# A ternary feed-forward kernel: w2 transposed by two DMAs in place of TensorE

## What is computed

```python
q_emb = relu(cond @ W3 + b3)                    # (128, 256)
v_sum = sum(x, axis=1, keepdims=True)           # over the 32 positions
c = relu((32 * x + v_sum) * q_emb[:, None, :] @ W2 + b2)
def ternary_quant(w):                           # s: mean of |w| over the whole matrix
    return clip(round(w / s), -1, 1) * s
h1 = c @ ternary_quant(w1).T                    # w1, w3: 682 x 256
h3 = c @ ternary_quant(w3).T
out = x + (silu(h1) * h3) @ ternary_quant(w2).T # w2: 256 x 682
```

## Time and profile before

| what | value |
|---|---|
| median of 3 runs | 171.23 us (171.2 to 171.48) |
| the profiled execution's own time | 171.47 us |
| its span, first to last instruction | 169.3 us |
| granted TensorE clock, mean | 0.997 of full speed |
| busy share of the span: TensorE / VectorE / ScalarE / GpSimd | 97% / 67% / 51% / 23% |
| DMA: bytes, mean rate | 14.25 MB, 84 GB/s |

### The profile page before, as it was taken

How to read it: one execution, slowest core, us unless ns; L and a number is a source line. 1 busy time by engine, 2 the same in 40 slices (tenths; PEclk the granted TensorE clock), 3 DMA queues, 4 the chain that set the end, 5 groups by cost and what they waited for, 6 DMA issues and landing times.

```text
span 169.3 us, 2525 instructions
## 1 busy us (share of the span) xinstructions
PE 164.0 (97%) x918; PEld 139.3 (82%) x918; DVE 113.7 (67%) x182; ACT 87.0 (51%) x161; POOL 38.1 (23%) x38
## 2 busy tenths in 40 slices
PE   7799999999999999999999999999999999999993
PEld 2788778888788887888788887888788888888792
DVE  3239997774994399664994389664995359356763
ACT  4159876636553463635553463635553475255540
POOL 5000022731506042410506042410506030000000
PEclk9999999999999999999999999999999999999998
DMA  4998659964065002620056002100030003000303
GB/s 136 310 361 123 100 79 327 349 131 64 0 166 82 4 0 98 117 33 0 0 145 99 8 0 89 38 0 0 2 126 4 0 2 124 0 4 0 124 0 124
DMA packets 36244, 14.25 MB, mean 84 GB/s; under 512 B 25904, under 2 KB 35976, under 8 KB 36232
## 3 DMA queue, kind: packets, MB, share of 16 engines
q1 hardware_dynamic: 35944, 13.90, 31.7%
q10 hardware_dynamic: 288, 0.20, 0.4%
HBM read 9.90 MB, written 4.19 MB: 83 GB/s over the span
## 4 chain that ended last, share of the span: by engine, by line
PE 93%; DMA 2%; SPq 1%; ACT 1%; DVE 1%; issue 0%; ACTq 0%
PE bank L464 48%; PE bank L493 25%; PE bank L394 17%; DMA xo<-in_x_dram 2%; PE bank L380 2%; PE bank L418 0%; PE bank L400 0%; DVE x L545 0%; ACT silu L343 0%; ACT T L304 0%; DVE xo L656 0%; SPq L195 0%; SPq L190 0%; SPq L192 0%; PE bank L406 0%
## 5 line engine op out<-in xcount | busy, mean ns | idle before, releaser
L464 PE MATMUL bank<-c_hi,T 128*128 128x512 f32 (+1 forms) x176 | 71.0, 403 | 0.2 <-ACT T L308 0.2
L464 PE MATMUL bank<-c_lo,T 128*128 128x512 f32 (+1 forms) x176 | 69.4, 394 | 0.0
L343 ACT ACTIVATE silu<-bank,checked 128x512 f32<-128x512 f32 (+1 forms) x48 | 33.0, 688 | 67.0 <-PE bank L464 67.0
L643 DVE TENSOR_TENSOR gf<-silu,bank 128x512 f32<-128x512 f32 (+1 forms) x48 | 32.8, 683 | 41.4 <-PE bank L464 32.4
L464 PEld LDWEIGHTS bank<-c_hi,T 128*128 128x128 f32 (+1 forms) x176 | 32.8, 186 | 6.8 <-ACT T L308 0.6
L464 PEld LDWEIGHTS bank<-c_lo,T 128*128 128x128 f32 (+1 forms) x176 | 32.8, 187 | 6.3
L253 POOL TENSOR_TENSOR c_lo<-ct,c_hi 128x512 fp32r<-128x512 f32 x12 | 20.6, 1714 | 71.2 <-ACT c_hi L294 71.2
L493 PE MATMUL bank<-T,g_hi 128*128 128x256 f32 x160 | 33.7, 289 | 0.0
L493 PE MATMUL bank<-T,g_lo 128*128 128x256 f32 x160 | 32.6, 281 | 0.0
L394 PE MATMUL bank<-x,W_sb 128*128 128x256 f32 x128 | 30.9, 384 | 0.1
L650 DVE TENSOR_TENSOR g_lo<-gf,g_hi 128x512 fp32r<-128x512 f32 x40 | 31.0, 776 | 0.0
(11 more groups left out here) (60 smaller groups left out, 75.1 us busy)
## 6 DMA issues: line engine op xcount, KB each, us to landing
out_dram<-xo SPq DMA_DIRECT2D x15, 256.0 KB, 2.3
xb<-in_x_dram SPq DMA_DIRECT2D x48, 64.0 KB, 2.6
xo<-in_x_dram SPq DMA_DIRECT2D x6, 512.0 KB, 8.1
w_sb<-in_L_ffn_w_dram SPq DMA_DIRECT2D x2, 640.0 KB
xo<-in_x_dram SPq DMA_DIRECT2D x4, 256.0 KB, 4.5
w_sb<-in_L_ffn_w_dram SPq DMA_DIRECT2D x1, 682.0 KB, 9.4
W_sb<-in_L_cond_W_dram SPq DMA_DIRECT2D x1, 256.0 KB, 3.2
out_dram<-xo SPq DMA_DIRECT2D x2, 128.0 KB, 2.1
```

Of the source, the lines that this page charges most:

```text
L343: nc.scalar.activation(silu[r, m % 2, :], h1[j % 2][r], ACT.Silu, scale=checked[r, 0:1]).then_inc(silu_done, 1)
L464: last = pe.matmul(dst[j % 2][0:w, :], T13[:, k, col:col + w], part[:, g % NC, k, :], start=(i == 0), stop=(i == len(passes) - 1))
L643: nc.vector.tensor_tensor(gf[r, m % 3, :], silu[r, m % 2, :], second, ALU.mult).then_inc(g_done, 1)
```

## The change

`transpose_w2` goes from TensorE. ScalarE issues two DMAs with transposition in its place (`turn_w2`), one for each half of the 256 outputs, right behind the signs of w1 and w3 and ahead of `silu_step(1)`. They read `w2_t`, now padded to 768 columns, and write `w2_T`, a new buffer in SBUF. GpSimd clears the 86 columns of the padding once, early. `signs_of_T2` waits for both DMAs, reads `w2_T` in three activations, not four, and stands behind `hi_step(1)`, not behind `hi_step(0)`. `above_w2_limit` is `above_limit` for the padded buffer, with as many elements.

```diff
@@ -71,7 +71,9 @@
         w2_sb = sb("w2_sb", [P, DC, H], F32)
         w1_t = sb("w1_t", [P, STEPS, D], BF16)
         w3_t = sb("w3_t", [P, STEPS, D], BF16)
-        w2_t = sb("w2_t", [P, DC, H], BF16)
+
+        w2_t = sb("w2_t", [P, DC, STEPS * P], BF16)
+        w2_T = sb("w2_T", [P, STEPS, D], BF16)
         abs_sums = sb("abs_sums", [P, 3], F32)
         scales = sb("scales", [P, 3], F32)
         limits = sb("limits", [P, 3], F32)
@@ -123,7 +125,6 @@
 
         w13_ps = [[bank[:, 2 * k + part, :].bitcast(BF16)[:, 0:DC * PART * P].rearrange("p (c n) -> p c n", c=DC)
                    for part in range(2)] for k in (1, 2)]
-        w2_ps = [bank[:, 4 + b, :].bitcast(BF16) for b in range(2)]
 
         def mixed_of(n):
             return bank[:, 0 if n % 2 else 6, :]
@@ -148,7 +149,7 @@
         ternary_done = sem("ternary_done")
         checked_done = sem("checked_done")
         early_hi_done, early_lo_done = sem("early_hi_done"), sem("early_lo_done")
-        wT_done = sem("wT_done")
+        w2_filled, w2_turned = sem("w2_filled"), [sem(f"w2_turned{c}") for c in range(DC)]
         part_done = sem("part_done")
         T1_copied, T3_copied, T2_copied = sem("T1_copied"), sem("T3_copied"), sem("T2_copied")
         mixed_done, xT_done, vsum_done, y_done, x1_done = sem("mixed_done"), sem("xT_done"), sem("vsum_done"), sem("y_done"), sem("x1_done")
@@ -239,6 +240,7 @@
             nc.gpsimd.tensor_copy(ident16[:], ident[:]).then_inc(const_ready, 1)
             nc.gpsimd.memset(ones[:], 1.0).then_inc(const_ready, 1)
             nc.gpsimd.memset(T2[:, HC, :].bitcast(F32), 0.0).then_inc(zeroed, 1)
+            nc.gpsimd.memset(w2_t[:, :, H:STEPS * P], 0.0).then_inc(w2_filled, 1)
             nc.gpsimd.memset(g_rest[:].bitcast(F32), 0.0).then_inc(zeroed, 1)
 
             def scale_by_q(n):
@@ -308,19 +310,19 @@
                     nc.scalar.activation(T13[:, :, rest:rest + HR2], w13_ps[k][part][:, :, whole * P:whole * P + HR2],
                                          ACT.Sign).then_inc(copied, 1)
 
+            def turn_w2():
+                act.wait_ge(ternary_done, 5)
+                act.wait_ge(w2_filled, 1)
+                for c in range(DC):
+                    act.dma_start(w2_T[:, :, c * P:(c + 1) * P], w2_t[:, c, :], transpose=True).then_inc(w2_turned[c], 16)
+
             def signs_of_T2():
-                act.wait_ge(wT_done, 1)
                 act.wait_ge(zeroed, 4)
-                nc.scalar.activation(T2[:, 0:W2_HALF, :],
-                                     w2_ps[0][:, 0:W2_HALF * D].rearrange("p (j d) -> p j d", d=D), ACT.Sign
-                                     ).then_inc(T2_copied, 1)
-                nc.scalar.activation(T2[:, W2_HALF:HC, :],
-                                     w2_ps[1][:, 0:(HC - W2_HALF) * D].rearrange("p (j d) -> p j d", d=D), ACT.Sign
-                                     ).then_inc(T2_copied, 1)
+                for c in range(DC):
+                    act.wait_ge(w2_turned[c], 16)
+                nc.scalar.activation(T2[:, 0:HC, :], w2_T[:, 0:HC, :], ACT.Sign).then_inc(T2_copied, 1)
                 for row in (0, HR2):
-                    nc.scalar.activation(T2[row:row + HR, HC, :],
-                                         w2_ps[1][0:HR, (HC - W2_HALF) * D:(STEPS - W2_HALF) * D], ACT.Sign
-                                         ).then_inc(T2_copied, 1)
+                    nc.scalar.activation(T2[row:row + HR, HC, :], w2_T[0:HR, HC, :], ACT.Sign).then_inc(T2_copied, 1)
 
             relu(0)
             abs_sum(0, w1_sb, got_w1, 32)
@@ -353,6 +355,7 @@
             silu_step(0)
             signs_of_T13(0, 1, T1_copied)
             signs_of_T13(1, 1, T3_copied)
+            turn_w2()
             for m in range(NG * STEPS):
                 if m + 1 < NG * STEPS:
                     silu_step(m + 1)
@@ -363,7 +366,7 @@
                 hi_step(m)
                 if n is not None:
                     hi_of_c(n)
-                if m == 0:
+                if m == 1:
                     signs_of_T2()
 
         @block.tensor
@@ -406,18 +409,6 @@
                         last = pe.transpose(w13_ps[k][part][:, c, j * P:(j + 1) * P],
                                             w_t[:, part * PART + j, c * P:(c + 1) * P], ident16[:])
                 last.then_inc(part_done, 1)
-
-            def transpose_w2():
-                pe.wait_ge(ternary_done, 5)
-
-                pe.wait_ge(T3_copied, 3)
-                for j in range(STEPS):
-                    rows = P if j < HC else HR
-                    for c in range(DC):
-                        col = (j % W2_HALF) * D + c * P
-                        last = pe.transpose(w2_ps[j // W2_HALF][0:rows, col:col + P], w2_t[:, c, j * P:j * P + rows],
-                                            ident16[:])
-                last.then_inc(wT_done, 1)
 
 
             pe.wait_ge(blank_ready, 1)
@@ -485,7 +476,7 @@
                 pe.wait_ge(g_lo_done, m + 1)
                 parts = [(g_hi[j], P), (g_lo[j], P)] if j < HC else [(g_rest, RM)]
                 if m == 0:
-                    pe.wait_ge(T2_copied, 4)
+                    pe.wait_ge(T2_copied, 3)
                 if j == 0:
                     pe.wait_ge(o_free[b], g + 1)
                 for i, (part, rows) in enumerate(parts):
@@ -512,7 +503,6 @@
             pe.wait_ge(T1_copied, 3)
             h1_step(1)
             h3_step(1)
-            transpose_w2()
             LAST = (NG - 1) * STEPS
             for m in range(NG * STEPS):
                 j = m % STEPS
@@ -589,6 +579,12 @@
                 nc.vector.scalar_tensor_tensor(out=flat_weight(w_t)[:, cols], in0=size_of[k][:, cols],
                                                scalar=limits[:, k:k + 1], in1=flat_weight(w_sb)[:, cols],
                                                op0=ALU.is_gt, op1=ALU.mult).then_inc(ternary_done, 1)
+
+            def above_w2_limit():
+                dve.wait_ge(limit_done, 3)
+                nc.vector.scalar_tensor_tensor(out=w2_t[:, :, 0:H], in0=size_of[2].rearrange("p (c h) -> p c h", c=DC),
+                                               scalar=limits[:, 2:3], in1=w2_sb[:], op0=ALU.is_gt, op1=ALU.mult
+                                               ).then_inc(ternary_done, 1)
 
             def check_scales(cols, step):
 
@@ -629,7 +625,7 @@
             above_limit(1, w3_sb, w3_t, parts[1])
             check_scales(slice(0, 1), 0)
             limit(2)
-            above_limit(2, w2_sb, w2_t, slice(0, DC * H))
+            above_w2_limit()
 
             def g_step(m):
                 g, j = m // STEPS, m % STEPS
```

## The result

| | before | after |
|---|---|---|
| median of 9 executions | 171.23 us (171.04 to 171.76) | 172.76 us (171.86 to 176.61) |
| ratio of the times, 95% interval | 1 | 1.0059 (1.0042 to 1.0076) |
| the profiled execution: time, span, mean granted clock | 171.47, 169.3, 0.997 | 176.61, 174.5, 0.989 |

The change makes the kernel slower. The executions after fall into two groups: five from 171.86 to 172.76 us with a clock of 0.998 or more, and four from 175.18 to 176.61 with 0.989 or 0.99. The ratio is of the first group alone, since executions with a lower clock are set apart as disturbed, though here the kernel brings the lower clock about itself, as the experiments show. The profile is of one of the four.

What follows compares the result with a forecast made beforehand. TensorE's time was taken as the kernel's time. The terms -0.99 + 0.23 + 0 + 0 = -0.76 us took the median 171.23 to 170.47, say 170.5; range 170.2 to 172.8, the forecast's own 170.2 to 170.9.

Steps and rivals of the forecast that it cites:

- rivals A: Transposing issues hold ScalarE longer, following 2.79 - I: within 0.2% of no change, chance 0.17; a loss beyond, chance 0.13.
- rival B: Transposed data land late, so TensorE waits 3.7 us at the first output product: +2.9 us, 174.1 us, chance 0.16.
- Term 1: TensorE's 12 transposes of w2 and the slow start of the first product behind them go: -0.99 us.
- term 2: GpSimd's x1 of half 4 is now just late for TensorE's weight load of `project_c(4)`: +0.23 us.
- Term 3: Two transposing issues on ScalarE, 0.95 us each, ahead of the silu of step 1: 0 cost at the value taken.
- I: Time the two transposing issues together hold ScalarE ahead of the silu of step 1, taken as 1.9 us.
- The rule 2.79 - I: TensorE's lead surviving at `project_c(5)` is the smaller of 0.76 and 2.79 - I us; it shrinks from I = 2.03.
- Term 4: Signs of w2 on ScalarE, ending at 28.34, stay hidden if both DMAs land by 26.92: 0 cost.
- the forecast's estimate by pieces: ScalarE's issue time scaled from an x block's 512 pieces to a transposing DMA's 768: 0.95 us each.

Runs made afterwards that it cites:

- experiment 2: Kernel after, with SyncE instead of ScalarE issuing both transposes, ahead of the x blocks of halves 6 and 7: 170.52 us against 171.37 before, ratio 0.9955.
- experiment 8: Kernel after, with the six x-group loads held until the first transposition has landed: 170.55 us against 171.56 for the kernel before, ratio 0.9954.
- experiment 1: Kernel after, with SyncE's six x-group loads held until both transposes have landed: 170.74 us against 171.37 for the kernel before, ratio 0.9966.
- experiment 9: Kernel after, with SyncE waiting for w2_t before the x blocks of half 7: 171.05 us against 171.56 for the kernel before, ratio 0.9975.
- Experiment 10: Kernel after with all six group loads held, plus a third transposing DMA on ScalarE into a spare buffer: 172.61 us against 171.44 before, ratio 1.0068.
- experiment 4: Kernel after, with ten 512-column products into an unused bank ahead of TensorE's wait for T2: six executions from 172.63 to 176.43 us.
- experiment 7: Kernel after, with only the last three of six x-group loads held until both transposes landed: median 173.53 us, executions from 170.61 to 180.44.
- experiment 5: Kernel after, with twenty 512-column products into an unused bank ahead of TensorE's wait for T2: median 175.07 us, five executions from 174.52 to 175.91.

## Why the prediction was wrong

The gain was forecast at 0.76 us and is a loss of 1.0 (171.23 x 0.0059) to 5 us. That the median, 172.76, still lies within 170.2 to 172.8 says nothing for the forecast: the range reached that far only to take in part of rivals A and B, and the forecast's own ended at 170.9. The case that came is rival B, held at 0.16.

- **Term 1, -0.99, and term 2, +0.23: right.** The load for `project_c(4)` was forecast at 25.41 and came at 25.42, late by GpSimd's x1. Where T2 is in time (experiments 2 and 8), the time falls by 0.77 and 0.79 us, the forecast's 0.76.
- **Term 3, the issues: each a third longer than forecast, the time that ScalarE is held nearly right.** Forecast 0.95 us each, measured 1.30; but the first begins 0.6 us before the engine is free, so I is 2.09 and not 1.9. That is past the 2.03 from which the lead shrinks. `g_step(2)` was forecast at 26.35 and came at 26.42. The rule 2.79 - I fits where T2 is in time or nearly so: experiment 1 (I 2.20) should keep 0.59 us and kept 0.58, experiment 8 (2.09) 0.70 and kept 0.79, experiment 9 (2.39) 0.40 and kept 0.43. These differences are smaller than the intervals; the waits of `project_c(5)` for x1 of half 5, 0.29, 0.17 and 0.34 us, are seen in the profiles, and there is none in experiment 2, where ScalarE is not held. Experiment 10 confirms the mechanism beyond.
- **Term 4, the landing: the step that failed.** "With 3.2 it lands at 26.2" took the landing of a load of its size for a transfer that was going to meet SyncE's 512 KB loads; these were put at nothing because their data are used later, though what counted was their packets. Measured 8.4 us after the issue, 31.2. Rival B had priced this from the longest block (7.6 us): landing at 30.6, T2 at 32.6, TensorE waiting 3.7 and so the output product 2.9 later than before. The profile shows its mechanism, each size a little larger: landing at 31.2, T2 at 33.3, a wait of 4.54 and the output product 3.72 late.
- **What made me hold B unlikely** was the sentence that the transposes' issue starts 1.7 us before the group loads. It compared the first transposition's issue with 23.73, SyncE's time in one execution. But it is the second that decides, issued at 22.79, and SyncE's time is the end of a backlog of 16 block loads: 22.43, 22.33, 22.52 and 23.50 in the profiles of the kernel after and of experiments 4, 7 and 5, where this part of the queue is the same. The distance is near zero and changes sign between executions.
- **The clock was left out.** No case held that a wait of over 4 us would cost more than itself; in the profiled execution it cost 1.5 us more.

The runs in order of that distance (first group load's issue minus the second transposition's issue), with the landing of the second transposition, one profile each:

| kernel | distance, us | second landing after its issue, us |
|---|---|---|
| half the loads held (7) | -1.00 | 8.6 |
| after | -0.36 | 8.4 |
| half filled (4) | -0.02 | 7.4 |
| wholly filled (5) | +0.98 | 4.5 |
| blocks late (9) | +1.10 | 3.9 |
| first landed (8) | +2.04 | 2.6 |
| all held (1) | +3.02 | 2.9 |
| all held, third issue (10) | +3.19 | 3.1 |

So the cause of the loss is shown: group loads that are issued before, or just with, the second transposition. It rests on experiments 1 and 8, which move nothing but these loads and turn the loss into a gain, in 12 executions each. How the landing falls with the distance is an order of single profiles. Why a transposition behind such loads waits for so long is not settled. In the profile after, ScalarE's DMA queue (q10) had moved 768 of the 1600 packets of the two transposes by 24 us. From 24 to 26 it moved 47, while the other queue went on (packets, MB, share of the 16 engines):

```profile
q1 hardware_dynamic: 590, 0.35, 85.2%
q10 hardware_dynamic: 47, 0.00, 1.9%
```

The Trainium skill ("DMA: Bandwidth & Descriptors", Queues, rings and completion order) says that each DMA engine goes round between the queues that it has work for, packet by packet. The counts of 24 to 26 us, 47 against 590, do not look like it. But from 26 to 28 us ScalarE's queue moved the more packets:

```profile
q1 hardware_dynamic: 270, 0.26, 66.0%
q10 hardware_dynamic: 532, 0.14, 55.2%
```

So ScalarE's queue stood nearly still for 2 us and then moved most of the second transposition. Whether the page's packet is what this view counts is not known, so the trace neither confirms nor refutes the rule.

## What to carry to other kernels

A short transfer on which an engine waits has to be issued before the bulk loads that would share the DMA engines with it, and the order has to be enforced: move it ahead in the same queue, or let the bulk loads wait (the versions of experiments 2 and 8 beat the kernel before by 0.45%, and the kernel after by more). A distance between two queues read from one profile is one draw; where the issue time is the end of a backlog, look at how it moves before resting a sum on it. And price a DMA's landing by the busiest row of its stretch, not by its size.

## What was not expected of the hardware

- A transposing DMA of 128 x 768 bf16 holds its sequencer for 1.27 to 1.56 us in all ten profiles that have one. The median block load holds it for 0.63, and the forecast's estimate by pieces was 0.95. With little traffic beside it, it lands in 2.6 us (experiment 2).
- The clock: in the kernel after, TensorE's queue waited 4.54 us, then ran for 0.8 us at 2.4 GHz, and then for 3.4 us at 1.2 GHz. In experiment 7 the lower clock was there from the first product behind a gap of 4.33 us. After an idle stretch of 1.06 us (experiment 4) it did not fall. Nor did it in the five executions of the kernel after that were at most 1.53 us above the median of before; their idle stretches have no trace.
- GpSimd's product of 128 x 512 took 1.49 us in place of 1.05 in one place of experiment 10, where it ran at another moment against VectorE's work. That this is the reason was not tested.
